# Exponent and high half head by head on ACT, the low half of head 1 between the next tile's maxima on DVE

## The chip, the cores and the metric

The kernel runs on one core of a Trainium2 chip. The metric is the device time of one execution in microseconds (us); the median of several runs is compared.

## The reference

Inputs are `x` (4 batches of 1024 rows and 1024 columns) and `cond_2048` (4 rows of 1024).

```python
scale, shift = jnp.split(scale_shift, 2, axis=-1)      # emb @ W_emb + b_emb
xn = _rms_norm(x, g_norm) * (1.0 + scale) + shift
qkv = xn @ W_qkv
...
q = _rms_norm(q, g_q)
k = _rms_norm(k, g_k)
logits = jnp.einsum('bhqd,bhkd->bhqk', q, k) * d ** (-0.5)
attn = jax.nn.softmax(logits, axis=-1)
o = jnp.einsum('bhqk,bhkd->bhqd', attn, v)
o = jnp.swapaxes(o, 1, 2).reshape(b, n, dim)
return o + o @ W_out
...
x = x + _L0_cond_ref(x, cond_2048[:, None, :], L0_cond_W_emb, ...)
x = x + _L1_cond_ref(x, cond_2048[:, None, :], L1_cond_b)
```

There are 16 heads of 64. The last line is a causal convolution along the rows, separate for each column, with four taps (`cond_2048`'s four rows), plus `b`.

## The kernel before

The work is cut into 32 **units** `u`: four batches by eight groups of two heads. A unit computes the attention of its two heads for all 1024 queries, in eight **tiles** `p` of 128 queries; each tile has a head `h` of 0 and one of 1, and slot `s = 2 * p + h`. While unit `u` does its attention, TensorE also projects q, k and v of unit `w = u + 1` (`project`, L1002, spread over tiles 0 to 4), and, from unit 8 on, makes the output product of block `T = u - 8` (`out_product`, L1036 and L1042, tiles 5 to 7), whose convolution DVE computes (`convolve`, L1673 to L1684). So units 0 to 7 have no output products, units 8 to 30 have everything, and unit 31 has no projection.

Numbers are carried as two f16 parts, a high half and a low half, and each product is three matmuls. For one head of one tile the chain is:

- TensorE: `score` writes 128 x 1024 scores (L946) into one half of the PSUM tile `scores`, which has a half for each head and no second buffer. It starts with a wait until both exponents of the tile before have read it (`exp_done`).
- DVE: `maximum`, the negated row maximum (L1531) and from it the exponent's bias (L1534).
- ACT: `exponent` (L1187) writes `prob` (part of the memory called `late`) and sums each row; `high` (L1195) makes the f16 high half in `p_pair`.
- DVE: `low` (L1540), `prob` less its high half, the f16 low half.
- SP: `transpose_p` (L750), a DMA that transposes both halves into `pT` for `attend` (L965), which multiplies with the values two tiles at a time.

Each engine runs its instructions in the order in which they are written out; semaphores hold them until their inputs are there. SP issues all DMAs in one order too: the two transposes of the tile before come first in each tile, and behind them the loads of the next projection's weights (`load_w`, L727) and the stores of results.

DVE's order within a tile is: both maxima, then work of the unit's other stages (inverse of the row sums `invert`, L1641 and L1644; `scale_values`, L1652; `sums` of squares for the norm of q and k, L1551 and L1554; `normalise` with the factors that GpSimd raises to a power in L1447, L1562 and L1566), then the two low halves:

```python
for p in range(K):
    maximum(u, p, 0)
    maximum(u, p, 1)
    ...
    low(u, p, 0)
    low(u, p, 1)
```

`square`, `stage`, `misc` and `proj` are buffers of the projection and the output product; `out_transposes` (L1054) on TensorE turns finished convolution blocks back.

Of the kernel before, what the change touches and what calls it, by code (L numbers as in the profile page):

```python
# [461 lines left out]
def main(nc, const, shared, w_dram, mod_dram, xn_dram, o_dram, x, W_qkv, W_out, out):  # L462
    B, N, D, K = dims(x, W_qkv)
    U = B * K
# [12 lines left out]
    with ExitStack() as ctx:  # L477
# [702 lines left out]
        def _(act):  # L1180
            def exponent(u, p, h, par):
                s = 2 * p + h
                act.wait_ge(bias_done, slot(u, s) + 1)
                need(act, lo_done, slot(u, s) - 1)
                if s % 4 == 0:
                    need(act, inv_done, NG * u + s // 4 - 7)
                nc.scalar.activation(prob[:, h, :], scores[:, h, :], ACT.Exp, bias=bias[:, s:s + 1],  # L1187
                                     scale=const["l_scale"][:, 0:1],
                                     accum_out=total[:, par * NS + s:par * NS + s + 1]).then_inc(exp_done, 1)
# [111 lines left out]
            def unit(u, par, qkv, xs, outs, fins):  # L1301
                w, v, T = u + 1, u + K, u - K
                begun = not (static(u) and u == 0)
                last = u + 1 == U
                for p in range(K):
                    if last and p == 2:
                        read_y(T, T - par + 2, 0)
                    if last and p == 4:
                        read_y(T, T - par + 2, 1)
                    if p % 2 == 1 and p >= 3:  # L1310
                        read_inverses(u, (p - 3) // 2)
                    elif p == 1 and begun:
                        read_inverses(u - 1, 3)
                    if p == 0:
                        if has_early(u):
                            read_projection(w, 1)
                        if fins:
                            read_y(T - 1, T + par, 1)
                        if xs:
                            x_square(v, par, 2, x_in[:], (x_ld, 16 * (u + 1)), pair[:, 1], (xT_in, 16 * u))  # L1320
                    if p in (1, 2, 3) and qkv and not has_early(u):
                        read_projection(w, (1, 2, 4)[p - 1])
                    if p == 5:
                        if qkv:
                            read_projection(w, 7)
                            squares(w, 1, (h_ss, 2 * w + 1))
                        if fins:
                            read_out(T - 1, 1)
                    if p == 6:
                        if outs and not last:  # L1330
                            read_y(T, T - par + 2, 0)
                        if qkv:
                            read_stacks(w, 1 - par, 0, 0, 0, misc[:])
                            read_stacks(w, 1 - par, 0, 1, 1, proj[:, 1, :])
                        if qkv and outs:
                            high_halves(w, 1)
                    if qkv and outs and p == 7:
                        read_stacks(w, 1 - par, 1, 1, 2, misc[:], k_ev)
                    if gives_early(u) and p == 7:
                        read_projection(w + 1, 0)  # L1340
                    exponent(u, p, 0, par)
                    exponent(u, p, 1, par)
                    high(u, p, 0)
                    high(u, p, 1)
                    if 4 <= u < K and p in (1, 3):
                        wo_high(2 * u - 8 + p // 2)
                    if qkv and not outs and p == 6:
                        high_halves(w, 1)
                    if p % 2 == 0 and p >= 4:
                        o_high(u, (p - 4) // 2)  # L1350
                    elif p % 2 == 0 and begun:
                        o_high(u - 1, 2 + p // 2)
                    if qkv and p == 7:
                        read_stacks(w, 1 - par, 1, 0, 3, proj[:, 0, :])
                    if p == 0 and qkv:
                        read_projection(w, 2 if has_early(u) else 0)
                    if p == 1 and has_early(u):
                        read_projection(w, 3)
                    if p == 1 and xs:
                        x_high(v, x_in[:], pair, (xT_in, 16 * u))  # L1360
                    if p == 2:
                        if fins:
                            read_out(T - 1, 0)
                        if qkv:
                            read_projection(w, 4 if has_early(u) else 3)
                            squares(w, 0, (x_lo, v + 1) if xs else (h_ss, 2 * w))
                    if p == 3 and qkv:
                        read_projection(w, 5)
                        high_values(w, 1 - par, 0)
                    if p == 4:  # L1370
                        if qkv:
                            read_projection(w, 6)
                        if outs and par == 0:
                            scaled_eye(T)
                        if qkv:
                            high_halves(w, 0)
                    if p == 5 and qkv:
                        high_values(w, 1 - par, 1)
                    if last and p == 5:
                        scaled_eye(U - K)  # L1380
# [145 lines left out]
        def _(dve):  # L1526
# [161 lines left out]
            def unit(u, par, qkv, xs, outs, fins):  # L1688
                w, v, T = u + 1, u + K, u - K
                begun = not (static(u) and u == 0)  # L1690
                last = u + 1 == U
                for p in range(K):
                    maximum(u, p, 0)
                    maximum(u, p, 1)
                    if p == 0:
                        if xs:
                            x_mean(v, par, 2)
                        if begun:
                            invert(u - 1, 3, 1 - par)
                    if p == 1:  # L1700
                        if fins:
                            convolve(T - 1, 1 - par, 0, 1)
                        if xs:
                            x_shift(v, x_in[:])
                    if p in (2, 4, 6):
                        invert(u, p // 2 - 1, par)
                    if p == 2:
                        if outs and par == 0:
                            set_scale(T)
                        if fins:  # L1710
                            convolve(T - 1, 1 - par, 1, 0)
                    if p == 3 and fins:
                        convolve(T - 1, 1 - par, 1, 1)
                    if p == 4 and qkv:
                        normalise(w, 0)
                    if p == 5 and qkv:
                        sums(w, 1)
                    if p == 6 and qkv and not outs:
                        normalise(w, 1)
                    if last and p == 5:  # L1720
                        set_scale(U - K)
                    if u in (1, 2) and p < 4:
                        wo_maximum(4 * u - 4 + p)
                    if u == 3 and p == 0:
                        wo_maxima()
                    if u == 3 and p == 2:
                        wo_scales()
                    if 4 <= u < K and p in (2, 4):
                        wo_lower(2 * u - 8 + p // 2 - 1)
                    if p == 7 and outs and not last:  # L1730
                        convolve(T, par, 0, 0)
                    elif p == 7 and qkv:
                        read_keys(w, 1 - par)
                    if p % 2 == 0 and p >= 4:
                        scale_values(u, (p - 4) // 2)
                    elif p % 2 == 0 and begun:
                        scale_values(u - 1, 2 + p // 2)
                    low(u, p, 0)
                    low(u, p, 1)
                    if p == 0 and xs:  # L1740
                        x_multiply(v, par, x_in[:])
                    if p == 3 and qkv:
                        sums(w, 0)
                    if p == 5 and qkv and outs:
                        normalise(w, 1)
# [56 lines left out]
            head_low(KH - 1, KH, h_hi, 2).then_inc(h_lo, 1)  # L1802
            read_keys(0, 0)
            in_units(unit, dve)
            invert(U - 1, 3, 1)
            scale_values(U - 1, 2)
            for T in range(U - K - 1, U):
# [27 lines left out]
```

## Time and profile before

| | |
|---|---|
| runs | 2456.92 us median of 3 (2450.82 to 2458.89) |
| profiled execution | 2456.85 us; span of its instructions 2454.9 us |
| TensorE matmul busy (PE) | 2337.2 us, 95% |
| TensorE weight load busy (PEld) | 1529.3 us, 62% |
| DVE | 2061.2 us, 84% |
| ACT | 1797.1 us, 73% |
| GpSimd (POOL) | 648.6 us, 26% |
| mean granted clock of TensorE | 0.992 |
| DVE low halves L1540 | 512, 616.4 us busy, 1245 ns each |
| ACT exponents L1187, high halves L1195 | 512 each, 1204 and 1046 ns each |

The shares are means over the whole span; which engine sets the time differs between the stretches and is read from them. A matmul's row reaches from its first column to the modelled end of its last, so two that follow each other overlap.

### The profile page before, as it was taken

The numbers are of one execution on the slowest core, as the hardware profiler recorded it, in microseconds if no ns is written. First come the engines' busy times: TensorE is split into PE (matmuls) and PEld (weight loads), VectorE is DVE, ScalarE is ACT, GpSimd is POOL, SyncE is SP. The second block draws the span as 40 slices with busy tenths as digits, with TensorE's granted clock in tenths as the row PEclk, the third lists the DMA queues.
The fourth block names the chain that finished last, engine by engine and source line by source line (L and its number), as shares of the span: only waits on it lengthen the run. The fifth ranks groups of instructions, "written<-read, shape, count | busy, mean of one in ns | idle before, by whom it ended". The sixth has DMA issues, their size and how long they took to land.

```text
span 2454.9 us, 53605 instructions
## 1 busy us (share of the span) xinstructions
PE 2337.2 (95%) x20666; PEld 1529.3 (62%) x20666; DVE 2061.2 (84%) x3239; ACT 1797.1 (73%) x2706; POOL 648.6 (26%) x451
## 2 busy tenths in 40 slices
PE   5799898988899999999999999999999999999899
PEld 0455555555466666666666666666666666666688
DVE  7768988888878898888888888888888888888876
ACT  5467788788777777777777787777777777777732
POOL 1122333333333222323322223233212222222100
PEclk9899999999999999999999999999999999999999
DMA  8989989899999999999999999999988998889971
GB/s 361 315 208 230 194 177 200 180 189 225 202 207 181 203 183 215 182 200 231 204 208 191 213 183 201 192 189 222 208 177 172 182 175 162 177 162 176 186 187 52
DMA packets 1234732, 484.94 MB, mean 198 GB/s; under 512 B 1139632, under 2 KB 1197872, under 8 KB 1232048
## 3 DMA queue, kind: packets, MB, share of 16 engines
q1 hardware_dynamic: 1234480, 481.53, 93.4%
q8 instruction: 164, 2.69, 0.5%
q14 instruction: 88, 0.72, 0.1%
HBM read 137.20 MB, written 56.66 MB: 79 GB/s over the span
## 4 chain that ended last, share of the span: by engine, by line
PE 72%; DVE 11%; SPq 4%; issue 3%; ACT 2%; DMA 2%; POOL 1%; ACTq 0%; POOLq 0%
PE proj L1002 32%; PE proj L1036 12%; PE scores L946 11%; PE values L965 11%; DVE p_pair L1540 4%; DVE neg L1531 4%; SPq L750 3%; PE proj L1042 2%; PE values L978 1%; ACT p_pair L1195 1%; DMA w_sb<-w_dram 1%; PE misc L1054 1%; PE misc L1014 1%; PE proj L1014 1%; SPq L706 1%
## 5 line engine op out<-in xcount | busy, mean ns | idle before, releaser
L1002 PE MATMUL proj<-w_sb,xn_sb 128*128 128x384 f16 x6144 | 1034.1, 327 | 26.4 <-DMA w_sb<-w_dram 18.2
L1002 PEld LDWEIGHTS proj<-w_sb,xn_sb 128*128 128x128 f16 x6144 | 592.8, 98 | 431.3 <-issue 50.4
L1187 ACT ACTIVATE late<-scores,bias,l_scale 128x1024 f32<-128x1024 f32 x512 | 615.9, 1204 | 332.6 <-DVE bias L1534 313.7
L1540 DVE TENSOR_TENSOR p_pair<-late,p_pair 128x1024 f16<-128x1024 f32 x512 | 616.4, 1245 | 173.5 <-ACT p_pair L1195 173.2
L1531 DVE TENSOR_REDUCE neg<-scores 128x1 f32<-128x1024 f32 x512 | 623.2, 1217 | 101.7 <-PE scores L946 98.7
L1195 ACT ACTIVATE p_pair<-late 128x1024 f16<-128x1024 f32 x512 | 510.0, 1046 | 0.0
L965 PE MATMUL values<-pT,v_pair 128*64 128x256 f16 x6144 | 385.3, 275 | 13.2 <-ACT inv_all L1255 13.2
L946 PE MATMUL scores<-late 64*128 64x512 f16 x3072 | 376.1, 378 | 18.1 <-ACT late L1187 17.6
L965 PEld LDWEIGHTS values<-pT,v_pair 128*64 128x64 f16 x6144 | 316.4, 110 | 91.8 <-issue 70.1
L1447 POOL TENSOR_TENSOR rs<-ms,power 128x16 f32<-128x16 f32 x63 | 183.1, 2906 | 400.2 <-DVE ms L1554 399.9
L1036 PE MATMUL proj<-late,wo 128*128 128x256 f16 x2304 | 267.5, 273 | 0.8 <-DMA late<-in_x 0.8
L1476 POOL TENSOR_TENSOR oT_pair<-oT,oT_pair 128x256 f16<-128x256 f32 x124 | 148.4, 1197 | 436.2 <-ACT oT_pair L1264 436.2
L946 PEld LDWEIGHTS scores<-late 64*128 64x128 f16 x3072 | 128.9, 94 | 197.8 <-issue 45.0
L1036 PEld LDWEIGHTS proj<-late,wo 128*128 128x128 f16 x2304 | 222.3, 98 | 30.4 <-issue 5.8
L1452 POOL TENSOR_TENSOR qk_pair<-stage,qk_pair 128x512 f16<-128x512 f32 x126 | 147.1, 1189 | 327.2 <-ACT qk_pair L1218 327.2
L1684 DVE SCALAR_TENSOR_TENSOR late<-late,taps 128x256 f32<-128x256 f32 x324 | 157.1, 485 | 11.6
L1255 ACT ACTIVATE inv_all<-values 128x256 f32<-128x256 f32 x128 | 48.9, 382 | 139.0 <-PE values L978 138.9
L1203 ACT ACTIVATE stage<-proj 128x384 f32<-128x384 f32 x256 | 123.0, 480 | 25.4 <-PE proj L1002 25.4
L1534 DVE TENSOR_SCALAR bias<-neg,l_scale 128x1 f32<-128x1 f32 x512 | 109.6, 214 | 18.1
L1472 POOL TENSOR_TENSOR pair<-x_in,pair 128x1024 f16<-128x1024 f32 x24 | 66.9, 2788 | 207.2 <-ACT pair L1249 199.7
L1187 ACT ACTIVATION_READ_ACCUMULATOR late<-scores,bias,l_scale 128x1 f32 x512 | 98.6, 193 | 0.0
L1036 PE MATMUL proj<-xn_sb,wo 128*128 128x256 f16 x744 | 86.5, 273 | 0.8 <-ACT late L1286 0.8
(178 smaller groups left out, 1939.2 us busy)
## 6 DMA issues: line engine op xcount, KB each, us to landing
w_sb<-w_dram SPq DMA_DIRECT2D x121, 384.0 KB, 4.1
o_dram<-oT_pair SPq DMA_DIRECT2D x124, 128.0 KB, 2.4
out<-late SPq DMA_DIRECT2D x54, 256.0 KB, 2.9
x_in<-in_x SPq DMA_DIRECT2D x25, 512.0 KB, 4.8
late<-in_x SPq DMA_DIRECT2D x25, 512.0 KB, 4.2
wq_raw<-in_L_cond_W_qkv SPq DMA_DIRECT2D x8, 1536.0 KB, 10.7
late<-o_dram SPq DMA_DIRECT2D x12, 1024.0 KB, 6.3
xn_dram<-late SPq DMA_DIRECT2D x21, 512.0 KB, 3.3
```

The lines of the kernel that those rows point to most:

```text
L946: last = nc.tensor.matmul(scores[:, h, n * HN:(n + 1) * HN], stack[rows_, par, i, p * P:(p + 1) * P], stack[rows_, par, j, n * HN:(n + 1) ...
L965: last = nc.tensor.matmul(values[DH * h:DH * h + DH, 0:QG].rearrange("p (a n) -> p a n", a=2), v_pair[:, par, 2 * c + h, DH * i:DH * i + D ...
L1002: last = nc.tensor.matmul(proj[:, t % 2, 0:6 * DH], xn_sb[:, t, i * K + c, :], w_sb[:, c, j, :], start=(c == 0 and i == j == 0), stop=(c = ...
L1036: last = nc.tensor.matmul(dst, const["wo"][:, c, b, m * P:(m + 1) * P], oT_[:, c, a, :], start=(c == 0 and a == b == 0 and c1 == K), stop= ...
L1187: nc.scalar.activation(prob[:, h, :], scores[:, h, :], ACT.Exp, bias=bias[:, s:s + 1], scale=const["l_scale"][:, 0:1], accum_out=total[:, ...
L1195: nc.scalar.activation(p_pair[:, s % 4, 0, :], prob[:, h, :], ACT.Copy).then_inc(hi_done, 1)
L1447: nc.gpsimd.tensor_tensor(rs[:], ms[:], const["power"][:, 0:4 * KH], ALU.pow).then_inc(h_pw, 1)
L1452: last = nc.gpsimd.tensor_tensor(qk_pair[:, j, 1].rearrange("p t (h d) -> p (t h) d", d=DH), stage[:, hf, :, j * DH:(j + 1) * DH], qk_pair ...
L1476: nc.gpsimd.tensor_tensor(o_half(u, g, 1), oT[:], o_half(u, g, 0), ALU.subtract).then_inc(o_low, 1)
L1531: nc.vector.tensor_reduce(neg[:, s:s + 1], scores[:, h, :], axis=AX.X, op=ALU.max, negate=True).then_inc(max_done, 1)
L1540: nc.vector.tensor_tensor(p_pair[:, s % 4, 1, :], prob[:, h, :], p_pair[:, s % 4, 0, :], ALU.subtract).then_inc(lo_done, 1)
L1684: nc.vector.scalar_tensor_tensor(out=acc_[:, m, :], in0=y_[:, m, k:k + QG], scalar=const["taps"][:, k, c:c + 1], in1=acc_[:, m, :], op0=AL ...
```

## The change

On ACT each head's high half follows that head's exponent. On DVE the low half of head 1 leaves the end of its tile and goes between the two maxima of the next tile (for the last tile, behind all units).

```diff
@@ ACT, unit @@
-                    exponent(u, p, 0, par)
-                    exponent(u, p, 1, par)
-                    high(u, p, 0)
-                    high(u, p, 1)
+                    for h in range(2):
+                        exponent(u, p, h, par)
+                        high(u, p, h)
@@ DVE, unit @@
                 for p in range(K):
                     maximum(u, p, 0)
+                    if p:
+                        low(u, p - 1, 1)
+                    elif begun:
+                        low(u - 1, K - 1, 1)
                     maximum(u, p, 1)
@@ DVE, unit @@
                     low(u, p, 0)
-                    low(u, p, 1)
@@ DVE, after the units @@
             in_units(unit, dve)
+            low(U - 1, K - 1, 1)
             invert(U - 1, 3, 1)
```

The order of DVE before, in a unit from 8 to 30, from the low halves of tile 5 to the first maximum of tile 7:

```order
L1540 TENSOR_TENSOR p_pair<-late,p_pair 128x1024 x2
L1562 TENSOR_TENSOR stage<-stage,rs 128x8x128
L1566 TENSOR_TENSOR stage<-stage,g_qk 128x8x64
L1531 TENSOR_REDUCE neg<-scores 128x1
L1534 TENSOR_SCALAR bias<-neg,l_scale 128x1
L1531 TENSOR_REDUCE neg<-scores 128x1
L1534 TENSOR_SCALAR bias<-neg,l_scale 128x1
L1641 RECIPROCAL inv<-total 128x4
L1644 COPY inv_wide<-inv 128x256
L1652 TENSOR_TENSOR oT<-values,inv_all 128x256
L1540 TENSOR_TENSOR p_pair<-late,p_pair 128x1024 x2
L1531 TENSOR_REDUCE neg<-scores 128x1
```

The same place in the changed kernel, whose lines on DVE are numbered one lower:

```order
L1539 TENSOR_TENSOR p_pair<-late,p_pair 128x1024
L1561 TENSOR_TENSOR stage<-stage,rs 128x8x128
L1565 TENSOR_TENSOR stage<-stage,g_qk 128x8x64
L1530 TENSOR_REDUCE neg<-scores 128x1
L1533 TENSOR_SCALAR bias<-neg,l_scale 128x1
L1539 TENSOR_TENSOR p_pair<-late,p_pair 128x1024
L1530 TENSOR_REDUCE neg<-scores 128x1
L1533 TENSOR_SCALAR bias<-neg,l_scale 128x1
L1640 RECIPROCAL inv<-total 128x4
L1643 COPY inv_wide<-inv 128x256
L1651 TENSOR_TENSOR oT<-values,inv_all 128x256
L1539 TENSOR_TENSOR p_pair<-late,p_pair 128x1024
```

One low half now stands ahead of the normalisation L1561 and of the next tile's first maximum, where two stood; the other, of head 1 of tile 5, stands behind that maximum's bias and ahead of the second maximum.

The order of ACT at tile 6 of the same unit, before:

```order
L1218 ACTIVATE qk_pair<-stage 128x512 x2
L1187 ACTIVATE late,total<-scores,bias,l_scale 128x1024 x2
L1195 ACTIVATE p_pair<-late 128x1024 x2
L1264 ACTIVATE oT_pair<-oT 128x256
L1255 ACTIVATE inv_all<-values 128x256
```

and in the changed kernel:

```order
L1218 ACTIVATE qk_pair<-stage 128x512 x2
L1187 ACTIVATE late,total<-scores,bias,l_scale 128x1024
L1195 ACTIVATE p_pair<-late 128x1024
L1187 ACTIVATE late,total<-scores,bias,l_scale 128x1024
L1195 ACTIVATE p_pair<-late 128x1024
L1264 ACTIVATE oT_pair<-oT 128x256
L1255 ACTIVATE inv_all<-values 128x256
```

The high half of head 0 (L1195) now stands ahead of the exponent of head 1 (L1187).

## Rows read from the trace of the kernel before

**Rows 1.** Stretch, length; PE, PEld, DVE, ACT, POOL busy; granted clock, DMA share, GB/s.

```profile
130.00:660.00 530.00, 473.22 (x4106) 279.26 (x4105) 449.12 (x612) 417.50 (x633) 162.93 (x113) 0.99 0.99 201
665.00:2280.00 1615.00, 1614.45 (x14588) 1075.74 (x14587) 1381.57 (x2156) 1237.52 (x1884) 457.54 (x307) 1.00 0.96 192
```

**Rows 2.** Waits of TensorE over the span: us in total, times, longest.

```profile
PE proj L1002 <- DMA w_sb<-w_dram: 18.2, 12, 3.9
...
PE scores L946 <- ACT late L1187: 17.6, 16, 1.9
```

**Rows 3.** Timeline of unit 15, TensorE: start, length, work, idle before it.

```profile
1213.51 1.47 PE L946 MATMUL scores<-late 64*128 64x512 f16 x12
...
1219.52 1.47 PE L946 MATMUL scores<-late 64*128 64x512 f16 x12
...
1226.69 0.98 PEld L946 LDWEIGHTS scores<-late 64*128 64x128 f16 x12 [0.21 <-ACT late L1187]
...
1229.54 6.99 PE L1002 MATMUL proj<-w_sb,xn_sb 128*128 128x384 f16 x42
```

**Rows 4.** The same timeline, DVE and ACT in tiles 6 and 7.

```profile
1215.01 1.22 DVE L1531 TENSOR_REDUCE neg<-scores 128x1 f32<-128x1024 f32 x1
...
1216.27 0.21 DVE L1534 TENSOR_SCALAR bias<-neg,l_scale 128x1 f32<-128x1 f32 x1
...
1216.40 1.22 DVE L1531 TENSOR_REDUCE neg<-scores 128x1 f32<-128x1024 f32 x1
1216.52 1.21 ACT L1187 ACTIVATE late<-scores,bias,l_scale 128x1024 f32<-128x1024 f32 x1 [0.27 <-DVE bias L1534]
...
1217.90 1.21 ACT L1187 ACTIVATE late<-scores,bias,l_scale 128x1024 f32<-128x1024 f32 x1
...
1219.10 1.99 ACT L1195 ACTIVATE p_pair<-late 128x1024 f16<-128x1024 f32 x2
...
1220.18 2.36 DVE L1540 TENSOR_TENSOR p_pair<-late,p_pair 128x1024 f16<-128x1024 f32 x2 [1.09 <-ACT p_pair L1195]
...
1225.34 1.21 ACT L1187 ACTIVATE late<-scores,bias,l_scale 128x1024 f32<-128x1024 f32 x1
```

**Rows 5.** The same timeline, sums, power and normalisation between tiles 5 and 6.

```profile
1208.80 0.23 DVE L1554 TENSOR_SCALAR ms<-ms,eps_u 128x16 f32<-128x16 f32 x1
1209.12 2.90 POOL L1447 TENSOR_TENSOR rs<-ms,power 128x16 f32<-128x16 f32 x1 [1.66 <-DVE ms L1554]
...
1213.12 1.22 DVE L1562 TENSOR_TENSOR stage<-stage,rs 128x1024 f32<-128x1024 f32 x1
...
1214.38 0.69 DVE L1566 TENSOR_TENSOR stage<-stage,g_qk 128x512 f32<-128x512 f32 x1
```

**Rows 6.** The same timeline, tile 1 of unit 16: scores, maximum, convolution, its transposes.

```profile
1236.46 1.47 PE L946 MATMUL scores<-late 64*128 64x512 f16 x12
...
1238.94 1.21 DVE L1531 TENSOR_REDUCE neg<-scores 128x1 f32<-128x1024 f32 x1
...
1242.35 1.53 DVE L1684 SCALAR_TENSOR_TENSOR late<-late,taps 128x256 f32<-128x256 f32 x3
...
1243.93 0.42 PEld L1054 LDWEIGHTS misc<-eye,late 128*128 128x128 f32 x4 [0.17 <-DVE late L1684]
```

**Rows 7.** Timeline of unit 31, scores of tiles 5 and 6 and DVE.

```profile
2325.97 1.47 PE L946 MATMUL scores<-late 64*128 64x512 f16 x12 [1.38 <-ACT late L1187]
...
2333.40 1.47 PE L946 MATMUL scores<-late 64*128 64x512 f16 x12 [1.87 <-ACT late L1187]
...
2334.32 2.36 DVE L1540 TENSOR_TENSOR p_pair<-late,p_pair 128x1024 f16<-128x1024 f32 x2 [2.07 <-ACT p_pair L1195]
```

**Rows 8.** SP's issues near tile 7 of unit 15, and the weight loads' median landing time.

```profile
1221.57 4.66 SPq L750 DMA_TRANSPOSE pT<-p_pair  x2
1226.35 0.66 SPq L727 DMA_DIRECT2D w_sb<-w_dram  x1
...
w_sb<-w_dram SPq DMA_DIRECT2D x121, 384.0 KB, 4.1
```

## The prediction

> **What bounds the kernel now.** I first read the busy time by stretch [rows 1]. From 665 to 2280 us, which holds units 9 to 30 and most of 8, TensorE is busy 1614.45 of 1615.00 us at a granted clock of 1.00. Between 130 and 660 us (units 0 to 7) it is busy 473.22 of 530.00. So in two thirds of the run any wait put on TensorE is paid in full, and nothing can be won there; only the ends have room.
>
> The list of TensorE's waits [rows 2] says of what that room is made: 17.6 us over 16 times for ACT's exponent (the score tile is single, so the next scores wait until head 1 has been read), and 18.2 us for projection weights. None of the exponent waits lies between 665 and 2280.
>
> Next I looked for the tile at which the exponent is nearest to being late. The time from one score group to the next is set by what TensorE does between them, and it is shortest from tile 6 to tile 7: 1213.51 to 1219.52, 6.01 us [rows 3]. Inside it the chain [rows 4] is: scores end at 1213.51 + 1.47 = 1214.98; maximum of head 0 at 1215.01; its bias at 1216.27; maximum of head 1 at 1216.40; exponent of head 1 from 1217.90 to 1217.90 + 1.21 = 1219.11; next scores at 1219.52. How close may these two come? At the next tile the exponent ends at 1225.34 + 1.21 = 1226.55 and the weight load of the scores starts at 1226.69 after a wait for it: 0.14 us. So tile 6 has 0.41 - 0.14 = **0.27 us to spare**, tile 7, whose maximum stood behind DVE's low halves, none. The gap after that, 1226.69 to 1236.46, is 9.77 us long, and the others of a unit are like it, so their chains have time to spare.
>
> **The change part by part.** No work is added or removed. DVE does the same 512 low halves and ACT the same 1024 passes; the question is only what each now stands in front of.
>
> *A low half between the two maxima.* Two low halves take 2.36 us [rows 4], so one takes 1.18. It stands before the maximum of head 1, so bias and exponent of head 1 come 1.18 us later than before, counted from the maximum of head 0. The high half that it needs was made a tile earlier, so it waits for nothing.
>
> *High half of head 0 before the exponent of head 1.* Two high halves take 1.99 us, one 1.00. After the exponent of head 0 (1216.52 + 1.21 = 1217.73) ACT now makes it, until about 1218.8 with a short wait for its own result; the exponent of head 1 can't start before 1217.90 + 1.18 = 1219.08 anyway. It is hidden by DVE's low half, with some 0.25 us to spare; without that cover it would cost up to 1.00.
>
> *Is the maximum of head 0 earlier in return?* A low half less stands in front of it, 1.18 us. Where the maximum waited for DVE, both effects cancel. In tile 6 it doesn't help: the maximum started 0.03 us after the scores ended [rows 3, 4]. It even gets a little later. Ahead of it stands the normalisation L1562, which needs GpSimd's power, which needs the sums that DVE makes after tile 5's second bias [rows 5]. That bias comes 1.18 us later too, so the sums' last step moves from 1208.80 to 1209.98, the power (starting 0.32 later, 2.90 long) ends at 1213.20 and not 1212.02, and L1562 can start at about 1213.3 where it started at 1213.12 behind the two low halves. L1566 then ends near 1215.2 and not at 1214.38 + 0.69 = 1215.07: about 0.15 us later, between 0 and 0.3, since spans on GpSimd are rough.
>
> So the scores of tile 7 start 1.18 - 0.27 + 0.15 = **1.06 us later** (0.9 to 1.2). TensorE is in order, so all behind them waits. There are 23 units with output products between these two tiles (8 to 30): 23 x 1.06 = **24.4 us** (21 to 28).
>
> *What is late next.* Tile 7: scores end at 1219.52 + 1.06 + 1.47 = 1222.05, the exponent of head 1 ends 0.03 + 4.10 + 1.18 = 5.31 later, where 4.10 is 1215.01 to 1219.11; with the 0.14 that is 1227.50. TensorE gets there at 1226.69 + 1.06 = 1227.75, so no second wait, by 0.25. Tile 1: TensorE's transposes L1054 start at 1243.93, right behind the convolution L1684 that ends at 1242.35 + 1.53 = 1243.88 [rows 6]. That convolution stands behind tile 1's second bias. Its end is 4.94 after the maximum at 1238.94; in the new order the maximum can start with the scores' end (1236.46 + 1.47 + 0.03 = 1237.96, shifted like TensorE), so the end comes at 1237.96 + 4.94 + 1.18 = 1244.08, and the transposes wait 0.05 more: 1244.13 against 1243.93, 0.2 us, in the 22 units 9 to 30: **4.4 us** (0 to 8).
>
> *Units 1 to 7.* The tiles whose exponent is waited for there start their maximum behind low halves, so -1.18 and +1.18 cancel; what is left is the later second bias of the tile before, which I estimate from that spare of about 0.25 as +0.25 per unit: **+2** (-4 to +6).
>
> *Unit 31.* No projections are left, and the chain alone sets the pace: 2325.97 to 2333.40, 7.43 us a tile, with DVE idle 2.07 us for the high half [rows 7]. In the new order the low half of head 0 fits behind the second bias, and the loop is 5.31 + 0.14 + 1.47 = 6.92. That is 0.51 less for about six tiles, 3 us; transposes stand in the same loop, so I take **-2** (-3 to 0).
>
> Sum: 24.4 + 4.4 + 2 - 2 = +28.8. The profiled execution took 2456.85 us, of which the span is 2454.9; the median of the runs is 2456.92, the same. That gives **2486 us**.
>
> **The rivals.**
>
> *Transposes and weights come late too* (0.10). Each second low half, and so its transpose, is later, and SP's queue is in order: the last quarter of the weights is issued behind the transposes of tile 6, at 1226.35 [rows 8]. Worked out as above, the low half of tile 6 ends at 1222.08 + 1.39 + 1.18 = 1224.65, its transpose takes 4.66 / 2 = 2.33, and the load goes out near 1227.2: 0.85 later, while TensorE is 1.06 later. It lands 4.1 us on, at 1231.3; the quarter is used 18 matmuls into the projection, 1229.54 + 1.06 + 18 x 0.166 = 1233.6. That holds by 2 us on the median load. But the issues are now closer together, and the weights were already waited for 12 times [rows 2]. If the load lands 3 to 4 us later, 1 to 2 us come on top in 23 units: 2510 to 2530.
>
> *TensorE makes the wait up* (0.06). If the busy time hid room, a late start would be caught up within the unit: the ends alone remain, 2457, no change. Against it: 42 matmuls of 384 columns take 6.99 us, 166 ns each [rows 3], and 384 columns at 2.4 GHz, the granted level, are 160 ns. The Trainium skill, "Perfetto Trace Analysis", section "Identifying the Most-Contended Engine", warns that matmul busy time is no measure of headroom and asks for the share of weight loads; that share is 1075.74 of 1615, or 67%, and by this rule a third would be free and the sum about 0. The trace's 166 ns speak against the rule here.
>
> *Faster* (0.07). The loop gains 0.51 us wherever it alone binds. At all 16 waits for the exponent [rows 2] that is -8.2 us: 2449. It decides only if the exponent of head 1 in tile 6 comes at most 0.27 us later, that is, if the low half costs a quarter of what its row says there.
>
> *The clock falls* (0.02). One gap of 1 us a unit is new. In 130 to 660 us TensorE was idle 56.78 us in all and the clock still 0.99 [rows 1]; at that mean the stretch of 1615 us would lose 16 us more: 2502.
>
> **How the numbers follow.** The forecast has 0.75 and its own range is 2471 to 2499, from the bounds of its terms (21 + 0 - 4 - 3 = 14 would be all lows at once, 28 + 8 + 6 = 42 all highs). The range that leaves out no more than 2 in 10 reaches somewhat into the weights' case: **2468 to 2506**. A measurement of this kernel tells about 0.3% (7 us) from no change. Faster 0.07, same 0.06, slower 0.87.
>
> **What the profile would show.** Right: between 665 and 2310 us a wait of TensorE's scores for ACT's exponent of about 1 us, some 23 times, all at tile 7, and the second maximum 2.57 us after the first. DVE no longer idle for the high half before L1540, without any gain. In unit 31 a tile in 6.9 us. Wrong would be: tile 7's scores on time (then the low half cost nothing, or the maxima overlap it), TensorE waiting for weights or for pT after 665 us (the DMA case), or a unit that takes no longer than before.

## The result

The changed kernel takes 2573.07 us (median of 4 runs, 2568.12 to 2575.95) against 2454.83 us of the kernel before (4 runs, 2450.82 to 2458.89): 1.0467 times as long, 95% interval 1.0445 to 1.0488. The direction is as forecast, the size is four times the forecast 28.8 us. The span of the profiled execution is 2566.3 us where it was 2454.9: **111.4 us more**, and this is the amount to be explained.

In the changed kernel the lines of DVE and GpSimd are lower by one: the maximum is L1530, the low half L1539, the normalisation L1561 and L1565, the power L1446. First the busy time by stretch, columns as in [rows 1]:

```profile
130.00:660.00 530.00, 479.25 (x4085) 283.82 (x4083) 453.79 (x607) 427.58 (x627) 166.54 (x110) 0.97 0.98 198
665.00:2280.00 1615.00, 1551.24 (x13676) 1021.33 (x13672) 1302.20 (x2024) 1195.95 (x1766) 438.12 (x287) 0.98 0.91 182
```

From 665 to 2280 us TensorE is now idle for 63.76 us, where it was idle for 0.55, and the clock's mean has fallen from 1.00 to 0.98. The list of TensorE's waits names the idle time; it answers to [rows 2]:

```profile
PE scores L946 <- ACT late L1187: 83.8, 42, 3.5
...
PE proj L1002 <- DMA w_sb<-w_dram: 11.8, 10, 2.5
PE values L965 <- DMA pT<-p_pair: 8.4, 3, 3.1
```

The wait is the forecast one, but up to 3.5 us long. To place it I took the time from one score group to the next in both traces, tile by tile. From tile 6 to tile 7 it is 3.6 us longer in unit 8, 2.86 in the odd units 9 to 29 and 3.15 in the even units 10 to 30: 3.6 + 11 x 2.86 + 11 x 3.15 = 69.7 us. From tile 7 to the next tile 0 it is 1.49 and 1.84 longer: 36.6 us. From tile 1 to tile 2 it is 0.17 longer, 22 x 0.17 = 3.7. Units 1 to 7 lose 7.4, unit 0 gains 2.1, unit 31 gains 2.2. The sum is 113.1; the remaining -1.7 lies in the other tiles, ahead of the first score group and behind the last.

The timeline of unit 16 shows why, from the scores of tile 5 to those of tile 7; it answers to [rows 3 to 5]:

```profile
1316.78 1.47 PE L946 MATMUL scores<-late 64*128 64x512 f16 x12
...
1323.78 0.23 DVE L1553 TENSOR_SCALAR ms<-ms,eps_u 128x16 f32<-128x16 f32 x1
1323.93 1.22 DVE L1539 TENSOR_TENSOR p_pair<-late,p_pair 128x1024 f16<-128x1024 f32 x1
...
1324.10 3.81 POOL L1446 TENSOR_TENSOR rs<-ms,power 128x16 f32<-128x16 f32 x1 [1.21 <-DVE ms L1553]
...
1327.01 1.47 PE L946 MATMUL scores<-late 64*128 64x512 f16 x12
...
1327.94 1.23 DVE L1561 TENSOR_TENSOR stage<-stage,rs 128x1024 f32<-128x1024 f32 x1 [2.79 <-POOL rs L1446]
...
1329.81 1.22 DVE L1530 TENSOR_REDUCE neg<-scores 128x1 f32<-128x1024 f32 x1
...
1331.15 3.25 POOL L1451 TENSOR_TENSOR qk_pair<-stage,qk_pair 128x512 f16<-128x512 f32 x2 [3.25 <-ACT qk_pair L1218]
1331.19 2.20 DVE L1539 TENSOR_TENSOR p_pair<-late,p_pair 128x1024 f16<-128x1024 f32 x1
...
1333.31 1.21 DVE L1530 TENSOR_REDUCE neg<-scores 128x1 f32<-128x1024 f32 x1
...
1334.81 1.20 ACT L1187 ACTIVATE late<-scores,bias,l_scale 128x1024 f32<-128x1024 f32 x1 [1.12 <-DVE bias L1533]
...
1336.16 2.74 PE L946 MATMUL scores<-late 64*128 64x512 f16 x12 [3.08 <-ACT late L1187]
```

The low half between the two maxima (1331.19) takes 2.20 us, not 1.18. GpSimd's first pass of its own low half (L1451) starts 0.04 us ahead of it. Two such passes took 2.27 us in the trace before, so one is over near 1332.3, and 1.1 us later DVE is done. The second maximum starts 3.50 us after the first, which was 1.39 [rows 4].

The first maximum is late as well: it starts 1.33 us after the scores' end, where it was 0.03. It stands behind the normalisation, that one behind the power, and the power takes 3.81 us where it took 2.90 [rows 5]: a low half of DVE started 0.17 us ahead of it. Before the change the normalisation waited for GpSimd once in the whole run, 3.0 us; now 24 times:

```profile
L1446 POOL TENSOR_TENSOR rs<-ms,power x63: 2898/2955/3812, 115.5 to 2381.8; 128x16 f32<-128x16 f32 x63
...
who waited for it (us, times):
  DVE stage L1561: 67.2, 24
```

The last row of the timeline has a third loss: tile 7's scores take 2.74 us and not 1.47. Three stretches of the same unit, columns as in [rows 1]:

```profile
1329.00:1333.00 4.00, 4.00 (x46) 3.43 (x40) 3.93 (x5) 2.81 (x5) 1.85 (x2) 1.00 0.53 110
1333.00:1336.10 3.10, 0.08 (x1) 0.00 (x0) 3.03 (x7) 1.98 (x3) 2.51 (x2) 0.92 0.48 92
1336.10:1339.50 3.40, 3.34 (x20) 1.39 (x21) 1.59 (x2) 1.49 (x4) 0.67 (x1) 0.57 1.05 216
```

TensorE is idle for 3.02 of 3.10 us, and in the 3.40 us after that the granted clock is 0.57, so mostly the lower level, 1.2 GHz and not 2.4. The trace's clock record falls 22 times like this between 665 and 2400 us, once in each of units 9 to 30, and not once before the change. Unit 8 has the longest wait, 3.53 us, and no fall; why is open.

At the end the forecast holds. In unit 31 a tile now takes 2439.57 - 2432.45 = 7.12 us, and the next 6.88, where it was 7.43 [rows 7]:

```profile
2432.45 1.47 PE L946 MATMUL scores<-late 64*128 64x512 f16 x12 [1.33 <-ACT late L1187]
...
2439.57 1.47 PE L946 MATMUL scores<-late 64*128 64x512 f16 x12 [1.07 <-ACT late L1187]
...
2446.45 1.47 PE L946 MATMUL scores<-late 64*128 64x512 f16 x12 [1.32 <-ACT late L1187]
```

**Theory**: DVE's low halves and GpSimd's passes hold each other up where the new order lays them side by side. That makes the wait at tile 7 three times as long as forecast, and the long gap costs TensorE its clock. **Rivals**: the order on ACT alone makes the loss; or the late transposes and weights; or the lost clock is no consequence of the gap.

The signs of the first part were in the trace of before, and I passed them over. It has these rows, of unit 3 and last of unit 15:

```profile
356.11 4.28 DVE L1540 TENSOR_TENSOR p_pair<-late,p_pair 128x1024 f16<-128x1024 f32 x2
...
356.46 2.85 POOL L1472 TENSOR_TENSOR pair<-x_in,pair 128x1024 f16<-128x1024 f32 x1 [7.50 <-issue]
...
1216.33 2.27 POOL L1452 TENSOR_TENSOR qk_pair<-stage,qk_pair 128x512 f16<-128x512 f32 x2 [4.32 <-ACT qk_pair L1218]
```

Two low halves take 4.28 us beside a pass of GpSimd, not 2.36; and in each of units 9 to 31 one low half, beside GpSimd's L1476, took 1.69 or 1.70 us. The last row is GpSimd's low half of q and k in tile 6: it already ran just where the change puts DVE's.

### The profile page after: what moved, and what is told of

The parts are those of the page before. It is cut to its first block, busy times and chain, and to the rows that moved or that the text cites. A ratio compares the mean times of both kernels' runs of the same rounds, so it can differ in the third digit from the quotient of the medians.

```text
span 2566.3 us, 53605 instructions
## 1 busy us (share of the span) xinstructions
PE 2386.5 (93%) x20666; PEld 1550.9 (60%) x20666; DVE 2078.3 (81%) x3239; ACT 1849.4 (72%) x2706; POOL 667.3 (26%) x451
## 4 chain that ended last, share of the span: by engine, by line
PE 65%; DVE 19%; POOL 5%; issue 3%; SPq 3%; DMA 2%; ACT 1%; POOLq 0%; ACTq 0%; DVEq 0%
PE proj L1002 34%; PE scores L946 12%; PE values L965 9%; DVE neg L1530 7%; DVE p_pair L1539 6%; PE proj L1036 5%; POOL rs L1446 4%; SPq L750 1%; DMA w_sb<-w_dram 1%; PE values L978 1%; DVE stage L1561 1%; DVE ms L1550 1%; PE misc L1054 1%; DVE bias L1533 1%; PE proj L1042 1%
## 5 line engine op out<-in xcount | busy, mean ns | idle before, releaser
L1002 PE MATMUL proj<-w_sb,xn_sb 128*128 128x384 f16 x6144 | 1034.1, 327 | 19.6 <-DMA w_sb<-w_dram 11.8
L1530 DVE TENSOR_REDUCE neg<-scores 128x1 f32<-128x1024 f32 x512 | 624.5, 1220 | 310.9 <-PE scores L946 310.5
L1187 ACT ACTIVATE late<-scores,bias,l_scale 128x1024 f32<-128x1024 f32 x512 | 615.4, 1202 | 281.6 <-DVE bias L1533 264.3
L1539 DVE TENSOR_TENSOR p_pair<-late,p_pair 128x1024 f16<-128x1024 f32 x512 | 666.1, 1301 | 2.9 <-ACT p_pair L1195 2.9
L1195 ACT ACTIVATE p_pair<-late 128x1024 f16<-128x1024 f32 x512 | 541.2, 1057 | 16.1
L946 PE MATMUL scores<-late 64*128 64x512 f16 x3072 | 400.6, 396 | 84.6 <-ACT late L1187 83.8
L965 PE MATMUL values<-pT,v_pair 128*64 128x256 f16 x6144 | 390.9, 278 | 15.4 <-DMA pT<-p_pair 8.4
L1446 POOL TENSOR_TENSOR rs<-ms,power 128x16 f32<-128x16 f32 x63 | 211.1, 3351 | 344.7 <-DVE ms L1553 343.9
L1451 POOL TENSOR_TENSOR qk_pair<-stage,qk_pair 128x512 f16<-128x512 f32 x126 | 172.9, 1393 | 330.1 <-ACT qk_pair L1218 330.1
L1475 POOL TENSOR_TENSOR oT_pair<-oT,oT_pair 128x256 f16<-128x256 f32 x124 | 105.5, 851 | 505.2 <-ACT oT_pair L1264 505.2
L1561 DVE TENSOR_TENSOR stage<-stage,rs 128x1024 f32<-128x1024 f32 x63 | 77.0, 1222 | 67.2 <-POOL rs L1446 67.2
L1471 POOL TENSOR_TENSOR pair<-x_in,pair 128x1024 f16<-128x1024 f32 x24 | 51.0, 2126 | 238.8 <-ACT pair L1249 231.2
L1460 POOL TENSOR_TENSOR v_pair<-stage,v_pair 128x512 f16<-128x512 f32 x64 | 100.3, 1568 | 3.8 <-DVE qk_pair L1781 2.2
```

Of the source, the lines that this page charges most:

```text
L946: last = nc.tensor.matmul(scores[:, h, n * HN:(n + 1) * HN], stack[rows_, par, i, p * P:(p + 1) * P], stack[rows_, par, j, n * HN:(n + 1) ...
L965: last = nc.tensor.matmul(values[DH * h:DH * h + DH, 0:QG].rearrange("p (a n) -> p a n", a=2), v_pair[:, par, 2 * c + h, DH * i:DH * i + D ...
L1002: last = nc.tensor.matmul(proj[:, t % 2, 0:6 * DH], xn_sb[:, t, i * K + c, :], w_sb[:, c, j, :], start=(c == 0 and i == j == 0), stop=(c = ...
L1195: nc.scalar.activation(p_pair[:, s % 4, 0, :], prob[:, h, :], ACT.Copy).then_inc(hi_done, 1)
L1446: nc.gpsimd.tensor_tensor(rs[:], ms[:], const["power"][:, 0:4 * KH], ALU.pow).then_inc(h_pw, 1)
L1451: last = nc.gpsimd.tensor_tensor(qk_pair[:, j, 1].rearrange("p t (h d) -> p (t h) d", d=DH), stage[:, hf, :, j * DH:(j + 1) * DH], qk_pair ...
```

## The experiments

The table has the change from before in the time between score groups, as means of the odd and of the even units 9 to 30, the sum over units 1 to 7, and the falls of the clock between 665 and 2400 us.

| kernel | median us | ratio (95% interval) | tile 6 to 7 | 7 to 0 | 0 to 1 | units 1-7 | clock falls |
|---|---|---|---|---|---|---|---|
| changed | 2573.07 | 1.0467 (1.0445-1.0488) | 2.86 / 3.15 | 1.49 / 1.84 | -0.04 / 0.00 | 7.4 | 22 |
| act_only | 2467.2 | 1.0052 (1.0037-1.0067) | 0.70 / 0.69 | 0.16 / 0.17 | -0.08 / 0.00 | -1.8 | 1 |
| dve_only | 2569.34 | 1.0467 (1.0451-1.0483) | 2.43 / 2.72 | 1.47 / 1.60 | 0.14 / 0.00 | 13.5 | 21 |
| tile6_old | 2503.04 | 1.0203 (1.0188-1.0218) | 1.63 / 1.93 | -0.01 / -0.01 | 0.05 / 0.00 | 6.1 | 2 |
| fill_gap | 2542.14 | 1.0358 (1.0341-1.0376) | 2.86 / 3.15 | -0.01 / -0.01 | 0.45 / 0.29 | 6.9 | 0 |
| pool_waits | 2528.26 | 1.0293 (1.028-1.0307) | 1.88 / 2.17 | -0.01 / 0.43 | 0.69 / 0.37 | 7.6 | 5 |
| tile5_pool | 2491.75 | 1.0147 (1.0132-1.0162) | 0.87 / 0.87 | -0.01 / -0.01 | 0.61 / 0.35 | 4.5 | 0 |
| dve_56 | 2473.05 | 1.0073 (1.0058-1.0088) | 0.00 / 0.00 | 0.00 / 0.00 | 0.15 / 0.00 | 7.9 | 1 |

The kernel before took 2454.38 us beside act_only, dve_only, tile6_old and fill_gap, and 2455.71 us beside the others.

### act_only: ACT's new order alone

```diff
-                    exponent(u, p, 0, par)
-                    exponent(u, p, 1, par)
-                    high(u, p, 0)
-                    high(u, p, 1)
+                    for h in range(2):
+                        exponent(u, p, h, par)
+                        high(u, p, h)
```

> Only ACT's order is changed (exponent and high half head by head); DVE's order is that of the kernel before. Theory (the late scores of tile 7 come from DVE's side: the low half between the maxima, stretched beside GpSimd, and a normalisation that waits for GpSimd's power): ACT alone makes the exponent of head 1 in tile 6 later by one high half, about 1.03 us, of which 0.27 are spare, so 0.76 us in 23 units: +17, about 2472 us, with the clock at 1.00 between 665 and 2280 us. Rival (ACT's order is the cause): 2550 or more.

A loss of half a per cent. Unit 16, from tile 6's first maximum to tile 7's scores:

```profile
1287.07 1.22 DVE L1530 TENSOR_REDUCE neg<-scores 128x1 f32<-128x1024 f32 x1
...
1289.89 1.06 ACT L1195 ACTIVATE p_pair<-late 128x1024 f16<-128x1024 f32 x1
...
1290.86 1.19 ACT L1187 ACTIVATE late<-scores,bias,l_scale 128x1024 f32<-128x1024 f32 x1
...
1292.19 1.47 PE L946 MATMUL scores<-late 64*128 64x512 f16 x12 [0.63 <-ACT late L1187]
```

The exponent of head 1 starts 3.79 us after the first maximum, where it was 2.89 [rows 4]: 0.90 later, the price the prediction gave the high half without DVE's cover (up to 1.00). Less the 0.27 to spare, 0.63 are left, the wait in the last row. ACT's order alone isn't the loss.

### dve_only: DVE's new order alone

```diff
+                    if p:
+                        low(u, p - 1, 1)
+                    elif begun:
+                        low(u - 1, K - 1, 1)
...
-                    low(u, p, 1)
...
+            low(U - 1, K - 1, 1)
```

> Only DVE's order is changed; ACT makes both exponents and then both high halves, as before. Theory: the wait of tile 7's scores stays near 3 us and the clock still falls once a unit: 2555 to 2590 us. Rival (ACT's order is the cause): near 2455 us.

It has nearly the whole loss. In its tile 6 the low half takes 2.20 us as in the changed kernel. In tile 5 the power takes 2.90 us, since the low half comes in after it has begun, and the first maximum is 0.58 (odd units) and 0.87 us (even) later than before, rather than 1.01 and 1.30. So the loss is DVE's order; ACT's adds 0.43 us a unit to it at tile 6, since high halves that are ready earlier let the low half in ahead of the power.

### tile6_old: tile 5's second low half back to the end of tile 5

```diff
-                    if p:
+                    if p and p not in (6,):
                         low(u, p - 1, 1)
-                    elif begun:
+                    elif p == 0 and begun:
                         low(u - 1, K - 1, 1)
...
+                    if p + 1 in (6,):
+                        low(u, p, 1)
```

> The changed kernel, but in every unit the low half of head 1 of tile 5 stays at the end of tile 5, so that nothing stands between the two maxima of tile 6. Theory: of the 3 us wait, the low half's own part (0.9) and its stretch beside GpSimd (1.0) go, the late normalisation (1.3) stays or grows a little: 1.1 to 1.9 us in 23 units, no fall of the clock, about 2480 to 2505 us. Rival A (the low half between the maxima is all of it): near 2455 us. Rival B (what makes tile 7 late lies elsewhere): 2560 or more.

Moving one low half of sixteen in a unit takes 70 us off (2573.07 to 2503.04). What stays at tile 7 is the late normalisation and ACT's high half, now without cover: 1.02 + 0.90 - 0.27 = 1.65, against 1.63 measured in the odd units. The gap is shorter and the clock fell twice, not 22 times: both falls lie at tile 7 of units 7 and 8, none in units 9 to 30. Unit 16 again:

```profile
1306.48 3.81 POOL L1446 TENSOR_TENSOR rs<-ms,power 128x16 f32<-128x16 f32 x1 [1.21 <-DVE ms L1553]
...
1310.32 1.23 DVE L1561 TENSOR_TENSOR stage<-stage,rs 128x1024 f32<-128x1024 f32 x1 [1.14 <-POOL rs L1446]
...
1317.32 1.47 PE L946 MATMUL scores<-late 64*128 64x512 f16 x12 [1.86 <-ACT late L1187]
```

### fill_gap: the changed kernel with matmuls that nobody reads in the gap

```diff
+                    if outs and not last and p == 7:
+                        pe.wait_ge(h_ev, 3 * w + 1)
+                        for _ in range(24):
+                            nc.tensor.matmul(misc[:, 0:QG], const["eye16"][:],
+                                             const["eye16"][:, 0:1].to_broadcast([P, QG]), start=True, stop=True)
                     score(u, p, par)
```

> The changed kernel, with 24 matmuls of 256 columns (about 2.6 us, into a PSUM tile that nobody reads then) ahead of tile 7's scores in units 8 to 30: TensorE works on nothing while it waits. Theory (the wait of 3 us makes the granted clock fall to half for 3.4 us, which costs 1.3 to 1.6 us more a unit): the wait's end stays, the clock stays at 1.00, about 33 us less than the changed kernel, 2535 to 2545 us. Rival (tile 7 is slow for another reason, transposes or weights): 2570 us as the changed kernel.

It adds work and is faster than the changed kernel. Unit 16, TensorE from tile 6 to tile 7:

```profile
1322.86 1.47 PE L946 MATMUL scores<-late 64*128 64x512 f16 x12
...
1328.77 2.83 PE L1094 MATMUL misc<-eye 128*128 128x256 f16 x24
1332.02 1.47 PE L946 MATMUL scores<-late 64*128 64x512 f16 x12 [0.42 <-ACT late L1192]
```

Tile 7's scores come 9.16 us after tile 6's, as in the changed kernel (1336.16 - 1327.01 = 9.15), but they take 1.47 us and not 2.74, and the clock didn't fall. So TensorE's idle time in the gap is what brings the fall about. The price by the spans is 2566.3 - 2539.9 = 26.4 us, by the medians 30.9. It is less than the 36.6 us between tile 7 and tile 0, since now 0.45 and 0.29 us come on top between tiles 0 and 1, where TensorE waits for weights (17.6 us over 19 times in the run, 11.8 over 10 in the changed kernel).

### pool_waits: GpSimd's low half of q and k waits for DVE's

```diff
+                        if outs:
+                            pool.wait_ge(lo_done, slot(u, 11) + 1)
```

The line stands ahead of L1451 in the changed kernel; slot 11 is head 1 of tile 5.

> The changed kernel; in units 8 to 30 GpSimd's low half of q and k (its first pass reads SBUF for 1.16 us) also waits until DVE's low half between the maxima of tile 6 is done. Theory (that low half takes 2.20 and not 1.22 us because GpSimd's pass started 0.04 us before it and DVE waits for it to end): the low half takes 1.2, tile 7's scores wait 1.9 to 2.2 us and not 2.85 to 3.15, and at such a wait the clock stays up: 23 x (1.0 + 1.4) = 55 less, near 2515; if the clock falls all the same, near 2550. Rival (the low half is slow for another reason, the transposes' DMA reads of the same tile): 2.20 stays, 2570 us.

In tile 6 of unit 16 the two no longer lie side by side:

```profile
1320.72 1.22 DVE L1532 TENSOR_REDUCE neg<-scores 128x1 f32<-128x1024 f32 x1
...
1322.10 1.22 DVE L1541 TENSOR_TENSOR p_pair<-late,p_pair 128x1024 f16<-128x1024 f32 x1
...
1323.23 1.22 DVE L1532 TENSOR_REDUCE neg<-scores 128x1 f32<-128x1024 f32 x1
...
1323.39 2.27 POOL L1451 TENSOR_TENSOR qk_pair<-stage,qk_pair 128x512 f16<-128x512 f32 x2 [4.58 <-DVE p_pair L1541]
```

The low half takes 1.22 us, the maxima are 2.51 us apart and not 3.50, and the time from tile 6 to 7 falls by 0.98, in odd and even units alike. So of the 2.11 us that the maxima moved apart, 1.13 is the low half and 0.98 GpSimd's pass. The total is 13 us above what was expected, for two reasons: the clock still fell five times (four at tile 7, of units 8, 18, 26 and 30, one behind a wait for weights of 2.34 us), and 0.69 and 0.37 us came back between tiles 0 and 1, with weights waited for 17 times, 23.2 us in all. That part of the weights' rival exists; why these loads land later here wasn't tested.

### tile5_pool: pool_waits, and tile 4's second low half back to the end of tile 4

```diff
-                    if p:
+                    if p and p not in (5,):
                         low(u, p - 1, 1)
-                    elif begun:
+                    elif p == 0 and begun:
                         low(u - 1, K - 1, 1)
...
+                    if p + 1 in (5,):
+                        low(u, p, 1)
```

> As the one before (GpSimd waits), and in every unit the low half of head 1 of tile 4 stays at the end of tile 4, so that tile 5's maxima, and with them the sums and GpSimd's power, keep their old times and the power doesn't start beside a low half. Theory (the late normalisation comes from the sums behind tile 5's second bias and from the power held up by a low half): tile 6's maximum is on time, and what is left is one uncontended low half less the spare, 0.9 us in 23 units, the wait that the prediction had: 2478 to 2488 us. Rival (the normalisation is late for another reason): 2515 us as the one before.

Both meetings with GpSimd are gone in this one:

```profile
1297.21 2.90 POOL L1446 TENSOR_TENSOR rs<-ms,power 128x16 f32<-128x16 f32 x1 [0.70 <-DVE ms L1555]
...
1301.61 1.47 PE L946 MATMUL scores<-late 64*128 64x512 f16 x12
1303.11 1.23 DVE L1532 TENSOR_REDUCE neg<-scores 128x1 f32<-128x1024 f32 x1 [1.01 <-PE scores L946]
...
1304.50 1.21 DVE L1541 TENSOR_TENSOR p_pair<-late,p_pair 128x1024 f16<-128x1024 f32 x1
1305.64 1.22 DVE L1532 TENSOR_REDUCE neg<-scores 128x1 f32<-128x1024 f32 x1
...
1308.49 1.47 PE L946 MATMUL scores<-late 64*128 64x512 f16 x12 [0.81 <-ACT late L1187]
```

The power takes 2.90 us, the first maximum starts 0.03 us after the scores, the second 2.53 us later (forecast 2.57), and tile 7's scores are 0.87 us late in odd and even units alike; without the 0.15 for the normalisation the prediction has 1.18 - 0.27 = 0.91. The clock doesn't fall. So tile 6 here has what the prediction worked out for it, a low half that nothing holds up and a maximum on time. The time, 2491.75 us, lies 3.75 us above the range expected for this run and 5.75 us above the forecast 2486; the wait for weights between tiles 0 and 1 (11 x 0.61 + 11 x 0.35 = 10.6 us) is the part that wasn't in the sum.

### dve_56: DVE's new order except ahead of tiles 5 and 6, ACT's order old

The edit is that of tile6_old with `(5, 6)` in place of `(6,)`, without ACT's hunk.

> ACT in the order of before; DVE in the changed order but for tiles 5 and 6, whose maxima stand together with the low half of head 1 at the end of tiles 4 and 5. Theory: no wait of tile 7's scores is left, the clock stays up; 0.17 us in 22 units for the transposes of tile 1 stay, and the first units are as with DVE's order alone (+5 to +13): 2458 to 2472 us. Rival (tile 7 is late for a reason outside tiles 5 and 6): over 2490.

Nothing is left at tiles 6 and 7. What stays is 0.17 us at tile 1 (3.7 us), 1.6 us between tiles 0 and 1, 1.1 us in unit 31 and 7.9 us in units 1 to 7; the time lies 1 us above the range that was expected. Where TensorE has idle time anyway, DVE's new order still loses.

### unit31_only: the kernel before with both new orders in unit 31 alone

The edits are those of act_only and dve_only, with `u == U - 1` as a condition.

> The kernel before, with both changed orders in unit 31 alone, where the chain alone sets the pace. Theory: the loop there is 0.55 us a tile shorter where it binds, 2 to 3 us in the unit, and nothing else moves: ratio 0.998 to 1.000, unit 31's eight tiles 2.2 us shorter in the profile. Rival (the gain is given back behind the unit by the transposes): no change of the span.

It took 2452.66 us against 2455.71, ratio 0.9991 (0.998 to 1.0001): not told apart from no change. Its unit 31 is 0.75 us shorter, where it gained 2.2 in the changed kernel. The difference is its first tile, 0.89 us longer than before and not 0.56 shorter. There DVE's two maxima still follow each other, since the low halves ahead of them are in the old order, and so ACT's high half has no cover, as in act_only:

```profile
2291.99 1.22 DVE L1533 TENSOR_REDUCE neg<-scores 128x1 f32<-128x1024 f32 x1
...
2293.38 1.21 DVE L1533 TENSOR_REDUCE neg<-scores 128x1 f32<-128x1024 f32 x1
...
2295.78 1.19 ACT L1187 ACTIVATE late<-scores,bias,l_scale 128x1024 f32<-128x1024 f32 x1
...
2297.12 1.47 PE L946 MATMUL scores<-late 64*128 64x512 f16 x12 [1.18 <-ACT late L1187]
```

The exponent of head 1 starts 3.79 us after the first maximum, the same figure as there.

No version beat the kernel before by a measurable amount.

## Why the prediction was wrong

**Right**: the place and the mechanism. TensorE's scores wait for ACT's exponent at tile 7 in each of the 23 units, the 0.27 us to spare hold, and the wait is paid in full. The transposes of tile 1 cost 0.17 us (forecast 0.2), unit 31 gained 2.2 us (forecast 2), and the high half is hidden under DVE's low half: the exponent of head 1 starts 1.50 us after the second maximum (1334.81 - 1333.31), as it did before (1217.90 - 1216.40).

**Mis-sized, the term "a low half between the two maxima"**: 1.18 us in the sum, 2.11 on the chip. The step that failed is "it waits for nothing". It waits for no semaphore, but GpSimd's pass takes up 0.98 us of its time. This was not an accident of timing: in tile 6 both start from the end of the normalisation, GpSimd by way of ACT's L1218 (1329.92), DVE by way of the maximum (1329.81), so they meet unit after unit: the low half takes 2.19 or 2.20 us in all 23. pool_waits takes that 0.98 away.

**Mis-sized, the normalisation**: 0.15 us (0 to 0.3) in the sum, 1.01 and 1.30 on the chip. I moved the sums by one low half and kept 2.90 us for the power. The low half now starts just ahead of the power, which takes 3.81; and the low half of tile 4 between tile 5's maxima is itself stretched beside GpSimd, to 1.56 or 1.57 us in the even units from 10 on and to 1.27 or 1.28 in the odd ones, so that the sums come later than forecast too; this is the difference between 1.30 and 1.01. tile5_pool puts both back, and the maximum is 0.03 us late as before.

The two together make the wait at tile 7: 1.30 + 2.11 - 0.27 = 3.14 us in even units, where 3.15 was measured.

**The rival that came in as well, "the clock falls"**: it got 0.02 and 2502 us. Its price came from the mean clock of 130 to 660 us, where the gaps are shared out over many tiles. One gap of 3 us in a unit does more: 26.4 us by fill_gap's span. With gaps as long as forecast, as in tile5_pool, the clock stays, so this follows from the two sizes above.

**The other rivals**: the order on ACT alone costs 0.5%, not 4.7%. From unit 8 on, transposes and weights are no part of the changed kernel's loss (a single wait for w_sb, 0.24 us); but in tile 5 of units 1, 3 and 6 TensorE waits 8.4 us for pT, which it didn't before, while it waits 6.4 us less for w_sb in the whole run. Weights cost 0.35 to 0.69 us a unit in pool_waits and tile5_pool. "TensorE makes the wait up" is refuted: in tile5_pool the 0.87 us aren't caught up in the rest of the unit. The share of weight loads that the Trainium skill points to ("Perfetto Trace Analysis", section "Identifying the Most-Contended Engine") was no room here. "Faster" would have needed a low half at a quarter of its price; it cost nearly twice.

**Units 1 to 7**: 7.4 us against a forecast of 2 (-4 to 6). The list of tiles puts most of it between tiles 5 and 6, about 0.85 us in most units, and there too one low half in each unit is stretched, to 1.75 us. The clock falls ten times between 130 and 665 us, where it fell four times. The loss is 13.5 in dve_only and -1.8 in act_only, so it comes with DVE's order; how it divides between GpSimd, the clock, the waits for pT and the later second bias wasn't separated.

## What to carry to other kernels

When an instruction moves to another place, its duration from the old place is not its price: look at what the engines that aren't in the sum do at the new place, and search the trace for rows where the same two kinds of instruction already lie side by side. A move can also lengthen the work that it now stands beside, here GpSimd's power, and what waits for that. And a gap on a busy TensorE should be priced by itself and not by a mean over a stretch, since beyond its own length it can cost the clock of the work behind it.

## What the runs showed of the hardware

DVE's low half (two inputs of 1024 columns, f32 and f16) and GpSimd's passes over two inputs held each other up: 2.20 us instead of 1.22 for DVE when GpSimd started 0.04 us earlier, 3.81 instead of 2.90 for GpSimd when DVE started 0.17 us earlier. The Trainium skill has this, "SBUF — State Buffer", section "Who interferes with whom": a DVE instruction with two inputs in SBUF contends with a GpSimd instruction that reads SBUF, and whichever comes second stands still. The durations agree: DVE ends 1.1 us after GpSimd's first pass is over, and the power takes 0.91 us more where the low half runs on for 1.05 us past its start. Of DVE's two-port modes the same page of the Trainium skill says that whoever issues first has the ports for the whole instruction. GpSimd's power held nothing for that long: in the trace before, 31 low halves lay beside a running power for 1.1 us or more, as the one of unit 15 from 1210.85 on beside the power of 1209.12 to 1212.02 [rows 5], and each took 1.22 or 1.23 us. So the power can be held up at its start but, once running, didn't hold DVE up. The maxima aren't held up: the one at 1216.40 [rows 4] lay beside GpSimd's L1452 of 1216.33 and took 1.22 us as ever.

TensorE's clock fell in each of units 9 to 30 of the changed kernel, which have an idle time of 2.79 or 3.08 us ahead of tile 7, but not in unit 8, with 3.53 us. In the same units it fell at tile 7 three times in pool_waits (with 2.10 us each), and never in tile6_old (1.57 or 1.86 us) and tile5_pool (0.81 us).
